# A rounding ladder in place of int8 casts, and a feed-forward stage in pairs of token tiles

## The reference

```python
xn = layernorm(x)
Q, K, V = xn @ W_Q, xn @ W_K, xn @ W_V
attn = softmax(causal(Q @ K.T / 32)) @ V          # one head, 1024 wide
def act_quant(x):                                  # per token
    scale = 127.0 / clip(max(abs(x), -1), 1e-5)
    return clip(round(x * scale), -128, 127) / scale
def weight_quant(w):                               # one scale for the matrix
    scale = 1.0 / clip(mean(abs(w)), 1e-5)
    return clip(round(w * scale), -1, 1) / scale
h = act_quant(xn) @ weight_quant(w1).T             # 1024 -> 4096
h = silu(conv1d(h, conv_w, kernel 3 along tokens, per channel) + conv_b)
ffn = act_quant(h) @ weight_quant(w2).T            # 4096 -> 1024
return x + attn + ffn
```

## Time and profile before

| what | us |
|---|---|
| median of the two runs shown | 5562.9 |
| lowest, highest | 5539.84, 5585.95 |
| the profiled execution, its time | 5550.48 |
| its span on the slowest core (core 6) | 5548.9 |
| spans of the eight cores | 5500.9 to 5548.9 |
| PE, DVE, ACT, POOL busy | 2210.5, 2351.0, 1049.0, 196.5 |

### The profile page before, as it was taken

One profiled execution on the slowest core, in us unless ns is written; L12 is line 12 of the kernel. 1 busy time (PEld: TensorE's weight loads), 2 busy tenths in 40 slices (PEclk: granted clock), 3 DMA queues, 4 the chain that ended last, 5 costly groups with the idle time before them and its releaser, 6 DMA issues.

```text
span 5548.9 us, 48211 instructions; the slowest of 8 cores (5500.9 to 5548.9 us)
## 1 busy us (share of the span) xinstructions
PE 2210.5 (40%) x15675; PEld 1301.9 (23%) x15675; DVE 2351.0 (42%) x4573; ACT 1049.0 (19%) x2539; POOL 196.5 (4%) x326
## 2 busy tenths in 40 slices
PE   1117885766665011223324334233242342432423
PEld 1113332323332010212312213122132231221322
DVE  6770002121211565645454454544544545445345
ACT  1112221111111000031221221312213122122131
POOL 0000000000000100000000000000000000000000
PEclk9999996677777555566666667666666676666766
DMA  7762123000001424200000000000000000000000
GB/s 66 63 61 59 63 86 100 21 18 16 12 12 25 136 87 172 86 14 12 24 12 22 14 12 23 14 13 23 12 22 14 12 24 12 18 19 12 23 13 8
DMA packets 100740, 202.61 MB, mean 37 GB/s; under 512 B 43568, under 2 KB 60048, under 8 KB 96400
## 3 DMA queue, kind: packets, MB, share of 16 engines
q0 software_dynamic: 37440, 149.15, 11.7%
q1 hardware_dynamic: 63056, 50.37, 4.0%
HBM read 149.13 MB, written 50.35 MB: 36 GB/s over the span
## 4 chain that ended last, share of the span: by engine, by line
PE 37%; DVE 35%; ACT 9%; issue 9%; DMA 8%; DVEq 1%; POOL 0%; ACTq 0%; POOLq 0%; SPq 0%
PE psM L1009 9%; PE psM L834 7%; PE psPV L555 5%; DVE h L883 5%; DVE q0s L875 5%; ACT q0s L860 5%; PE psS L478 4%; PE pj L341 4%; DVE h L968 3%; DMA sxb<-row_s 2%; DMA scr<-w 2%; DVE scr L904 2%; DVE mnbuf L904 2%; ACT h L890 2%; PE pj L382 2%
## 5 line engine op out<-in xcount | busy, mean ns | idle before, releaser
L860 ACT ACTIVATE q0s<-h,cwt 128x128 f32<-128x128 f32 x1024 | 326.8, 389 | 2359.3 <-DVE h L847 1662.7
L1009 PE MATMUL psM<-w2qT,ihb 128*128 128x512 bf16 x2048 | 514.2, 419 | 322.6 <-DVE r2c L1018 322.6
L834 PE MATMUL psM<-ixw,w1qT 128*128 128x130 bf16 x8192 | 546.2, 234 | 206.5 <-DVE h L847 206.5
L934 PE MATMUL psX<-identf,scr 128*128 128x128 f32 x32 | 14.3, 447 | 1497.0 <-DVE scr L927 1497.0
L834 PEld LDWEIGHTS psM<-ixw,w1qT 128*128 128x128 bf16 x8192 | 538.8, 105 | 218.6 <-issue 211.2
L875 DVE SCALAR_TENSOR_TENSOR q0s<-h,cwt,q0s 128x128 f32<-128x128 f32 x1024 | 291.5, 346 | 331.1 <-ACT q0s L860 330.9
L847 DVE TENSOR_TENSOR h<-psM,sxb 128x390 f32<-128x390 f32 (+1 forms) x352 | 188.7, 551 | 534.7 <-DMA sxb<-row_s 272.6
L1009 PEld LDWEIGHTS psM<-w2qT,ihb 128*128 128x128 bf16 x2048 | 214.3, 106 | 616.1 <-issue 420.5
L934 PEld LDWEIGHTS psX<-identf,scr 128*128 128x128 f32 x32 | 5.8, 182 | 1501.8 <-issue 1501.8
L867 ACT ACTIVATE q2s<-h,cwt 128x128 f32<-128x128 f32 x1024 | 323.0, 386 | 0.0
L883 DVE SCALAR_TENSOR_TENSOR h<-q0s,cbt,q2s 128x128 f32<-128x128 f32 x1024 | 292.4, 349 | 45.7 <-DVE q0s L875 45.5
(11 more groups left out here) (124 smaller groups left out, 2727.7 us busy)
## 6 DMA issues: line engine op xcount, KB each, us to landing
scr<-w POOLq DMA_DIRECT2D x64, 512.0 KB, 4.2
scr<-w POOLq DMA_DIRECT2D x32, 1024.0 KB, 5.6
xin<-x POOLq DMA_DIRECT2D x32, 512.0 KB, 12.1
xres<-x POOLq DMA_DIRECT2D x32, 512.0 KB, 4.1
out<-xres SPq DMA_DIRECT2D x32, 512.0 KB, 2.9
ixw<-ixT_s POOLq DMA_DIRECT2D x32, 260.0 KB, 3.7
ixT_s<-ixstg SPq DMA_DIRECT2D x32, 256.0 KB, 14.0
qT_s<-spst SPq DMA_DIRECT2D x64, 128.0 KB, 1.9
```

Source lines behind the costliest of these rows:

```text
L834: P.emit("tensor", (lambda hc_, q_, di_, ps_, sl_: lambda t: t.matmul(ps_[:, 132 * q_:132 * q_ + 130], w1qT[:, H * di_ + 128 * hc_:H * di_ ...
L860: P.emit("scalar", (lambda hc_, q_: lambda s: s.activation(out=q0s[:, 128 * q_:128 * (q_ + 1)], in_=h2[:, 132 * hc_:132 * hc_ + 128], func ...
L1009: P.emit("tensor", (lambda hc_, hf_: lambda t: t.matmul(psM2[:, 512 * hf_:512 * (hf_ + 1)], ihb[:, 128 * hc_:128 * (hc_ + 1)], w2qT[:, 102 ...
```

## The change

1. `SAFE_ROUND` becomes True: both roundings are computed by the ladder instead of the casts.
2. The feed-forward stage runs over 16 pairs of tiles. The first projection is done for 256 tokens at once: per chunk 8 matmuls of 2 x 130 columns (the two halves overlap by two tokens), one chunk per bank, four banks; ixw and sxb hold 258 tokens, h2 holds both halves (260 columns per chunk).
3. Then each half by itself: the convolution in four groups of eight chunks, with the intermediate products in two regions of scr16. ACT multiplies the left neighbour, and the right one with the bias added (Identity with bias and scale columns); DVE adds the two, multiplies the centre by its weight, and adds.
4. The folds use scr16 as well. The rounding is done in four pieces of 1024 columns. The bf16 result alternates between two halves of ihb; the f32 scratch of the ladder is always scr16[:, 0:1024]. After each piece PE does the 16 matmuls of its eight chunks.
5. The loads of xres and ares for tile tau + 2 are issued at the end of tile tau. The mask is made at the start of the attention stage. psW shares a bank with psX in the preparation of the weights, and some small tensors share space. Debug outputs that are never taken are left out below.

```diff
-SAFE_ROUND = False
+SAFE_ROUND = True
...
-        h2 = eD(nc.sbuf_tensor("h2", [128, HC * 132], F32))
-        ihb = eD(nc.sbuf_tensor("ihb", [128, HC * 128], BF16))
+        h2 = eD(nc.sbuf_tensor("h2", [128, HC * 260], F32))
+        ihb = eD(nc.sbuf_tensor("ihb", [128, 2 * 1024], BF16))
...
-        psM1 = [eD(nc.psum_tensor(f"psM1{k}", [128, 396], F32)) for k in range(3)]
+        psM1 = [eD(nc.psum_tensor(f"psM1{k}", [128, 260], F32)) for k in range(4)]
...
+        for pr in range(NPAIR):
+            sl = pr % 2
+            if pr + 1 < NPAIR:
+                ixready[pr + 1] = ixload(pr + 1)
...
+            for hc in range(HC):
+                pslot = hc % 4
+                ps = psM1[pslot]
...
+                for din in range(C):
+                    rhs = bass.AP(ixw[sl][:].tensor, 258 * din,
+                                  [[C * 258, 128], [128, 2], [1, 130]])
+                    P.emit("tensor", (lambda hc_, di_, ps_, rhs_: lambda t: t.matmul(
+                        bass.AP(ps_[:].tensor, 0, [[260, 128], [130, 2], [1, 130]]),
+                        w1qT[:, H * di_ + 128 * hc_:H * di_ + 128 * (hc_ + 1)], rhs_,
+                        start=(di_ == 0), stop=(di_ == C - 1)))(hc, din, ps, rhs),
+                        waits=mmw if din == 0 else (), inc="t" if din == C - 1 else None)
...
+            for half in range(2):
+                tau = 2 * pr + half
...
+                for qi in range(4):
+                    c0 = 8 * qi
+                    reg = qi % 2
+                    A0 = 2048 * reg
+                    B0 = 2048 * reg + 1024
+                    need = deq_pts[min(c0 + 7, HC - 1)]
+                    swq = [need, cw_ready] + scrA_guard[reg]
...
+                            func=ACT.Identity, bias=cbt[:, hc_:hc_ + 1],
+                            scale=cwt[:, 3 * hc_ + 2:3 * hc_ + 3]))(hc, q, B0, base),
...
+                    P.emit("vector", mkA(A0, B0), waits=[sq_done, P.now("v")], inc="v")
...
+                    P.emit("vector", mkB(c0, B0, base), waits=[P.now("v")], inc="v")
...
+                    P.emit("vector", mkC(c0, A0, B0, base), waits=[P.now("v")], inc="v")
+                    scrA_guard[reg] = [P.now("v")]
...
+                for qq in range(4):
+                    c0 = 8 * qq
+                    ring = qq % 2
...
+                        P.emit("vector", (lambda hq_: lambda v: v.tensor_tensor(
+                            out=hq_, in0=hq_, in1=s2rep, op=ALU.mult))(h2qA),
+                            waits=[s2b_ready, P.now("v")] + ([ihb_guard[ring]] if ihb_guard[ring] else []),
+                            inc="v")
+                        P.emit("scalar", (lambda hq_, b_: lambda s: s.activation(
+                            out=b_, in_=hq_, func=ACT.Sign, bias=halfcol[:],
+                            scale=1.0))(h2qA, bsl),
+                            waits=[P.now("v")], inc="s")
...
+                                P.emit("vector", (lambda cc_, b_: lambda v: v.scalar_tensor_tensor(
+                                    out=scr16[:, 0:1024], in0=b_, scalar=-cc_,
+                                    in1=scr16[:, 0:1024], op0=ALU.mult, op1=ALU.add))(cc, bsl),
+                                    waits=[P.now("s")], inc="v")
+                            P.emit("scalar", (lambda last, b_: lambda s: s.activation(
+                                out=b_, in_=scr16[:, 0:1024], func=ACT.Sign,
+                                bias=(0.0 if last else halfcol[:]), scale=1.0))(kk == 7, bsl),
+                                waits=[P.now("v")], inc="s")
...
+                scrA_guard[0] = [P.now("v"), m2done]
+                scrA_guard[1] = [P.now("v"), m2done]
```

More of the change, by code:

```diff
@@ L1016, in build_nc @@
-            m2done = P.now("t")
-            sg2 = -1.0 if safe else 1.0
-            P.emit("vector", (lambda sg_: lambda v: v.tensor_scalar(
-                out=r2c[:], in0=mx2c[:], scalar1=w2mc[:], scalar2=sg_ / 127.0,
-                op0=ALU.mult, op1=ALU.mult))(sg2),
-                waits=[w2mc_ready], inc="v")
-            aw = list(xaready[tau]) + [P.now("v")]
-            P.emit("vector", (lambda sl_: lambda v: v.tensor_tensor(
-                out=xres[sl_][:], in0=xres[sl_][:], in1=ares[sl_][:], op=ALU.add))(sl),
-                waits=aw, inc="v")
@@ L1026, in build_nc @@
-            ares_guard[sl] = P.now("v")
-            P.emit("vector", (lambda sl_: lambda v: v.scalar_tensor_tensor(
-                out=xres[sl_][:], in0=psM2[:], scalar=r2c[:], in1=xres[sl_][:],
-                op0=ALU.mult, op1=ALU.add))(sl),
-                waits=[P.now("v"), m2done], inc="v")
-            psM2_guard = P.now("v")
-            P.emit("sync", (lambda tau_, sl_: lambda sy: sy.dma_start(
-                out=out_d[128 * tau_:128 * (tau_ + 1), :], in_=xres[sl_][:]))(tau, sl),
-                waits=[P.now("v")], inc=f"ou{sl}", inc_n=16)
@@ new lines, in build_nc @@
+                m2done = P.now("t")
+                scrA_guard[0] = [P.now("v"), m2done]
+                scrA_guard[1] = [P.now("v"), m2done]
+                sg2 = -1.0 if safe else 1.0
+                P.emit("vector", (lambda sg_: lambda v: v.tensor_scalar(
+                    out=r2c[:], in0=mx2c[:], scalar1=w2mc[:], scalar2=sg_ / 127.0,
+                    op0=ALU.mult, op1=ALU.mult))(sg2),
+                    waits=[w2mc_ready, P.now("v")], inc="v")
+                aw = list(xaready[tau]) + [P.now("v")]
@@ new lines, in build_nc @@
+                P.emit("vector", (lambda osl_: lambda v: v.tensor_tensor(
+                    out=xres[osl_][:], in0=xres[osl_][:], in1=ares[osl_][:], op=ALU.add))(osl),
+                    waits=aw, inc="v")
+                ares_guard[osl] = P.now("v")
+                P.emit("vector", (lambda osl_: lambda v: v.scalar_tensor_tensor(
+                    out=xres[osl_][:], in0=psM2[:], scalar=r2c[:], in1=xres[osl_][:],
+                    op0=ALU.mult, op1=ALU.add))(osl),
+                    waits=[P.now("v"), m2done], inc="v")
@@ L1037, in build_nc @@
+                psM2_guard = P.now("v")
+                P.emit("sync", (lambda tau_, osl_: lambda sy: sy.dma_start(
+                    out=out_d[128 * tau_:128 * (tau_ + 1), :], in_=xres[osl_][:]))(tau, osl),
+                    waits=[P.now("v")], inc=f"ou{osl}", inc_n=16)
+                xres_guard[osl] = P.now(f"ou{osl}")
+                if tau + 2 < T:
+                    xaready[tau + 2] = xaload(tau + 2)
         P.emit("sync", None, waits=all_stores())
```

466 lines of the change are left out of this document (242 added, 224 removed).

## The result

| | us |
|---|---|
| changed kernel, median of 11 runs | 8681.3 (8619.8 to 8730.7) |
| kernel before, median of 10 runs now | 5621.5 (5526.6 to 5673.8) |
| ratio, 95% interval | 1.566 (1.557 to 1.574) |
| profiled execution: its time, span of core 3 (the slowest) | 8675.2, 8673.3 |
| spans of the eight cores | 8596.0 to 8673.3 |

A forecast was written before the change was run, and what follows sets the result against it. The prediction took a mostly serial chain across engines as the bound: 5548.9 + 2985 (feed-forward ladders) + 758 (normalization ladders) - 679 (pairs) = 8613 us of span, written as 8620, range 8480 to 8790.

The forecast's parts named there:

- Stand-ins: Ladder steps priced from other instructions' rows: 1225 ns for the DVE operation (L703), 1147 ns for Sign (Exp with bias).
- The normalization: Normalization of x: one ladder piece per tile, 25.1 us in place of 1.46; +23.7 per tile, +758 us over 32.
- The wait for sxb: Feed-forward, last DVE operation of a pair to first de-quantization: 12.4 us once per pair, against 10.1 per tile before.
- The other stages have the same instructions: Stages other than normalization and feed-forward: no added time, except the mask made again, under 1 us.
- the ladder piece: Feed-forward rounding: 25.6 us per 1024-column piece, four without overlap, 102.5 per tile against 9.2; +2985 us over 32 tiles.
- -679 us for the pairs: Feed-forward in pairs, without ladders: 139.0 us per pair against 181.4, so -42.4 per pair, -679 in all.
- three of four pieces are hidden: Second projection: PE's matmuls for three pieces run beside later pieces; 16 matmuls remain, 6.0 us per tile against 16.1.
- 1, table switches: ACT in both stages: Sign forces two table loads per tile, +165 us, 8780, or 8960 with drain; chance 6%.
- 2, the projection at the lower clock: Feed-forward's first projection stays at 1.2 GHz: +21 us per pair, +340, giving 8960; chance 3%.
- 3, no gain in the convolution: Feed-forward convolution stays at 60.4 us per pair instead of 45.6: +237, giving 8860; chance 3%.
- 4, a cheap ladder: Ladder steps about 0.3 us instead of 1.28, so kernel not slower, chance 1%; cheaper but still slower, 7350, 2%.
- 5, no ladder: The ladder is not reached in either stage, leaving the pairs' saving and smaller casts: 4850 us; chance 1%.

The follow-up runs named there:

- e1: The changed kernel with the int8 casts back in place of the ladder, pairs of tiles kept; 4986.4 us, ratio 0.898 to the kernel before.
- e2: The kernel before with the ladder switched on, over all 4096 columns at once, without pairs; 8710.1 us, ratio 1.568 to the kernel before.
- e4: The changed kernel with the ladders of two pieces interleaved, each with its own f32 scratch; 7366.1 us, ratio 1.325 to the kernel before.

## Why the prediction was right or wrong

**Right.** The stage is a chain, and every part of it came within 0.6 us of its forecast in the pair shown, and within 0.5 by the means (a single ladder piece counted as one part). Stand-ins were enough: Exp with a bias column for Sign, a weight-preparation step for the ladder's DVE operation, both to the nanosecond or two. The normalization was forecast at +23.7 us per tile; 36.15 per tile now (first to last L198: 15.5 to 1136.2 us over 31 tiles) against 12.47 is +23.7. The wait for sxb, forecast 12.4, was 12.5 by the mean of the stage; in the kernel before the same mean is 9.9. Of these 2.6 us, 0.9 are the issue of the larger ixw load, and 1.7 are left for its transfer, put at 1.4.

**The step that failed.** The mechanism held; what failed is the size of two terms, and both were too small. In the profiled executions the span grew by 3124 us (5548.9 to 8673.3), forecast were 3064. The 60 us lie here:

| stage, us | forecast | kernel before, core 6 | changed kernel, core 3 | growth less forecast |
|---|---|---|---|---|
| to the first matmul of the projections | +758 | 444.4 | 1200.4 | -2 |
| projections | 0 | 390.7 | 387.8 | -3 |
| attention | 0 | 944.9 | 991.7 | +47 |
| preparation of the weights | 0 | 564.2 | 551.4 | -13 |
| feed-forward | +2306 | 3204.7 | 5542.0 | +31 |

(The stages are cut at the first matmul of the projections, the first of the attention, the first load of the weights' preparation and the first matmul of the feed-forward stage.)

The first term was put at nothing: "The other stages have the same instructions" was taken to mean the same time on the core that sets the time. It took 47 us more in the attention. The cores that nothing disturbed show that the change is not its cause: 927 to 932 us on six cores of the changed kernel, 926 to 928 on four of the kernel before. On the others the granted clock was 0.81 for a part of the stage, by the clock records 422 us on core 3 of the changed kernel and 92 us on core 6 of the kernel before. 422 us at 0.81 in place of 1.00 would cost at most 422 x 0.19 = 80 us if PE were the bound all along (an estimate); core 3 took 60 longer than those six. So the base held a small disturbance of this kind and the result a larger one, and neither the sum nor its range had a term for it. What lowers the clock, no run here tells.

The second term is the ladder piece, put at 25.6 us: four of them take 103.5 us and not 102.5, which is +32 over 32 tiles. A step has a median of 2.571 us where 2.562 was put, 21 of the 768 steps between two L1044 of a piece are longer (up to 2.94 us), and the first operation of a tile's later pieces starts up to 0.17 us late. The other parts of the stage cancel (convolution 0.7 less per pair, SiLU and folds 0.4 more per tile). The eight cores took 5528 to 5569 us for the stage, forecast 5511. One price was worked out loosely and still came right: 8.80 us for 150 matmuls of 130 columns, doubled, are 0.117 us for 260 columns, the sum has 0.113, and the window above gives 22.20 / 199 = 0.112.

**A statement that was right only here.** The prediction carried -679 us for the pairs as a term of its own, and used it again for the rival without a ladder (4850). e1 refutes that: with casts the second projection is not hidden, the pairs save 569 us and the time is 4986. The step "three of four pieces are hidden" holds only while a piece takes longer on DVE and ACT than its matmuls on PE. And the sum hid that the ladder's own price depends on the width: beside the ladder over whole tiles (e2), pairs and pieces together save nothing measurable. The sum was right because both were priced in the form that they have in the changed kernel.

**The rivals.** 1, table switches: three loads in the trace, none at a Sign; it fell. The Trainium skill ("ScalarE: Activation LUTs", on table sets) says that cheap functions are in every set; by the trace Sign is one of them in the sets of Sqrt and of SiLU. 2, the projection at the lower clock: it runs at 1.00 after 3.8 us; fell. 3, no gain in the convolution: L917 takes 1225 ns and the first half 19.1 us; fell. 4, a cheap ladder: each step costs its row's price; fell. 5, no ladder: it is in every tile. Part of what the rival 4 asked for, two engines working at once, is what e4 builds: it gives back 1315 us, and even so that kernel takes 33% more than the kernel before.

## What to carry to other kernels

Price a chain of dependent operations by step and hop, and then ask whether two independent chains can share the two engines: interleaving gave 1315 us with the same instructions, where cutting the work into four narrow pieces run one after the other gave nothing. A piece that is meant to hide a matmul must take longer than the matmul; otherwise the wait turns round. Look at each queue for a small load that stands behind one which waits for a store: moving it gained 4% of the kernel before.

## What was not expected of the hardware

Two neighbouring cores of one execution ran the same attention instructions 60 us longer than the other six, at a mean granted clock of 0.70 against 0.77. The clock records of that execution have three values and not two: 0.50, 1.00 and 0.81. Cores 2 and 3 are at 0.81 for 407 and 422 us, all of it in the attention, cores 0 and 1 for 190 and 184 us, all of it in the feed-forward stage, and cores 4 to 7 never. It is not the change that brings it: in the profile of the kernel before cores 2, 3, 6 and 7 have 89 to 92 us of it in the attention, which takes 945 to 949 us there and 926 to 928 on the other four. In every trace the cores of a pair (0 and 1, 2 and 3, and so on) have it together, in amounts that differ by 63 us at most, and in two traces (e1, e2) no core has it. A difference of 20 to 70 us between cores or runs of one kernel here is thus no sign of what the kernel does, until the granted clock of the stage has been compared.

DVE and ACT, both working on f32 and bf16 tiles of SBUF at once through a whole ladder (e4), kept their durations to within 1%: 1223 ns instead of 1226 for DVE's step and 1148 instead of 1147 for ACT's.
